# A recurrent cell on one core: GpSimd forms one of the four sums over candidates by halves

## The chip, the cores and the metric

The kernel runs on one core of a Trainium2 chip. The metric is the device time of one execution in microseconds (us). The names of the engines in the profile are PE (TensorE), PEld (its weight loads), DVE (VectorE), ACT (ScalarE), POOL (GpSimd) and SP (SyncE).

## What is computed

A recurrent network runs over 2048 sequences of 256 steps. One step, cut to what matters here:

```
encoded   = tanh(x @ We + state @ Ue + be)
candidate = tanh(x @ Wx[c] + state @ Ws[c] + bk[c])        for c in 0..7, 32 values each
mem       = the last 20 of [encoded, err];  a = relu(mem @ enc_w1 + enc_b1)
h1, c1    = lstm(relu(a @ enc_w2 + enc_b2), h1, c1);  h2, c2 = lstm(h1, h2, c2)
gate      = softmax(h2 @ gate_w + gate_b) * theta + gate * (1 - theta)   (theta from the last 10 errors)
state     = sum over c of gate[c] * candidate[c]
pred      = clamp01(state[-1]);  err = pred - y
```

The change is about the line `state = sum over c`.

## The kernel before

The 2048 sequences are two groups of 1024. A group is eight tiles of 128 sequences, with the 128 on the partitions; a tile is named by a half `hf` (0, 1) and a quarter `q` (0 to 3). Two quarters make a `pair`. A phase works on three items at once: `new`, `cur` and `old`, an item being one step of one group, so 512 items in all. A loop of 51 turns has ten phases a turn. Each engine has its own program with the order of its calls written out by hand in `phase`, and the engines are tied by semaphores alone.

For an old item the new gate is made on VectorE (L781, L788), which writes it to PSUM, and a second time on GpSimd (L908), which writes it to SBUF. Then the products of gate and candidates are formed: VectorE multiplies the four tiles of pair 1 (`mix`, L799), GpSimd the four tiles of pair 0 in two instructions, quarter 1 and quarter 0 (`mix_quarter`, L920). The products lie in `mixed[partition, pair, hf, quarter in pair, 32, 8]` as float32. VectorE forms all four sums over the eight candidates (`mix_sum`, L817), each a reduction of 512 elements to 64 for one `hf` and one `pair`, into `state`. It does them between the parts of the current item's LSTM cells. The last part of its order in a phase reads: product of pair 1; sum (0, 1); first cell's terms (L720) and value (L726); sum (0, 0); the new hidden value in two instructions (L735); sum (1, 0); sum (1, 1); the sum of errors (L696); the second cell's terms (L720) and value (L726); theta (L702); the prediction (L825); the second cell's hidden value (L735); and the softmax.

L720, L726 and L735 read two tensors of SBUF each; L817 reads one; L799 reads one of SBUF and one of PSUM. ScalarE makes the gates' tanh (L561, L566) ahead of L720 and the tanh of the cell's value (L571) between L726 and L735.

TensorE waits for the first cell's hidden value (`q_h[0]`, set by the second L735) before the gate matmuls of the second cell (L417), then runs two history matmuls (L366) and transposes the state (`state_transpose`, L293): once for `hf` 0 and once for `hf` 1, each after the two sums of that half (`q_sum[hf][pair]`).

GpSimd's order in a phase is: gate (L908); product of quarter 1, of quarter 0 (L920); then for the current item `kept_share` (L886), which waits for theta, and `kept_gate` (L893); the new error and the prediction (L947, L956); the low part of the new entry (L926); the weighted exponentials (L900). Its products wait until the sums that read `mixed` pair 0 for the item before are done. GpSimd issues no DMA. The DMAs of the loop are issued from SyncE's queue.

Of the kernel before, what the change touches and what calls it, by code (L numbers as in the profile page):

```python
# [12 lines left out]
MEM, C, S, TRAJ, H, ENC = 20, 8, 32, 24, 16, 64  # L13
P = 128
GROUPS = 2
# [27 lines left out]
def recurrent_kernel(nc, x_l, y_l, y, error0, gate0, w, ident_c, columns_c, ind_c, out):  # L43
    ctx = ExitStack()
    with ctx:
        def sb(name, shape, dt=FP32):
            return ctx.enter_context(nc.sbuf_tensor(name, shape, dt))
# [4 lines left out]
        def sem(name):  # L52
            return ctx.enter_context(nc.semaphore(name))
# [37 lines left out]
        state = sb("state", [P, GROUPS, HF, Q, S])  # L91
# [10 lines left out]
        mixed = sb("mixed", [P, 2, HF, Q // 2, S, C])  # L102
# [36 lines left out]
        q_mulpool = [sem(f"q_mulpool{q}") for q in range(2)]  # L139
# [9 lines left out]
                                    "ring", "predout"))  # L149
        q_out_gate = [sem(f"q_out_gate{c}") for c in range(2)]  # L150
        q_in_high = sem("q_in_high")
        q_sum = [[sem(f"q_sum{hf}_{pair}") for pair in range(2)] for hf in range(HF)]

        block = ctx.enter_context(nc.Block())
# [468 lines left out]
        def _(dve):  # L623
# [186 lines left out]
            def mix_sum(item, hf, pair):  # L810
                g, n, u = item
                if pair == 1:
                    dve.wait_ge(q_mul[1], n + GROUPS)
                else:
                    for q in range(2):
                        dve.wait_ge(q_mulpool[q], n + GROUPS)
                V.tensor_reduce(state[:, g, hf, 2 * pair:2 * pair + 2, :], mixed[:, pair, hf, :, :, :], AX, ALU.add)\  # L817
                    .then_inc(q_sum[hf][pair], 1)
# [13 lines left out]
            def phase(items, extra):  # L832
                new, cur, old = items
                if old:
                    fresh_gate(old)
                    new_gate(old)
                if cur:
                    agent_input(cur, 1)
                if old:
                    mix(old, 1)  # L840
                    mix_sum(old, 0, 1)
                if cur:
                    cell_terms(cur, 0)
                    cell_value(cur, 0)
                if old:
                    mix_sum(old, 0, 0)
                if cur:
                    new_hidden(cur, 0, 0)
                    new_hidden(cur, 0, 1)
                if old:  # L850
                    mix_sum(old, 1, 0)
                    mix_sum(old, 1, 1)
                if cur:
                    error_sum(cur)
                    cell_terms(cur, 1)
                if new:
                    error_rows_wait(new, extra)
                if cur:
                    cell_value(cur, 1)
                    thetas(cur)  # L860
                if old:
                    prediction(old)
                if cur:
                    new_hidden(cur, 1, 0)
                    new_hidden(cur, 1, 1)
                if new:
                    errors(new)
                if cur:
                    peaks(cur)
                    below_peak(cur)  # L870
                    totals(cur)
                    reciprocals(cur)

            run_phases(dve, phase, turn_start)

        @block.gpsimd
        def _(pool):
            G = nc.gpsimd
            G.memset(hist[:, :, :, :].rearrange("p a k b -> p (a k b)").bitcast(FP32), 0.0).then_inc(s_hist0, 1)
            pool.wait_ge(s_ready, 1)  # L880
            pool.wait_ge(s_ys, 16)

            def kept_share(item):
                g, n, u = item
                pool.wait_ge(q_theta, n)
                G.tensor_tensor(one_theta[:, g, :], ones[:, :], theta[:, g, :], ALU.subtract)\  # L886
                    .then_inc(q_onetheta, 1)

            def kept_gate(item):
                g, n, u = item  # L890
                pool.wait_ge(q_onetheta, n)
                pool.wait_ge(q_keptfrom, n)
                G.tensor_tensor(kept[:, g, :, :], gate[:, g, :, :],  # L893
                                one_theta[:, g, :].rearrange("p (j o) -> p j o", o=1)
                                .to_broadcast([P, TILES, C]), ALU.mult).then_inc(q_kept, 1)

            def weighted_exponentials(item):
                g, n, u = item
                pool.wait_ge(q_exp, n)
                G.tensor_tensor(weighted[:, g, :, :], expd[:, g, :, :],  # L900
                                theta[:, g, :].rearrange("p (j o) -> p j o", o=1)
                                .to_broadcast([P, TILES, C]), ALU.mult).then_inc(q_weighted, 1)

            def gate_in_sbuf(item):
                g, n, u = item
                pool.wait_ge(q_fresh, n)
                pool.wait_ge(q_kept, n)
                G.tensor_tensor(gate[:, g, :, :], fresh[:, g, :, :], kept[:, g, :, :], ALU.add)\  # L908
                    .then_inc(q_keptfrom, 1)

            def mix_quarter(item, q):
                g, n, u = item
                pool.wait_ge(q_keptfrom, n + GROUPS)
                pool.wait_ge(q_cand[q], n + 1)

                for hf in range(HF):
                    pool.wait_ge(q_sum[hf][0], n + (GROUPS - 1))
                over_s = gate[:, g, q:Q:2, :].rearrange("p h (o c) -> p h o c", o=1)\
                    .to_broadcast([P, HF, S, C])
                G.tensor_tensor(mixed[:, 0, :, q, :, :], cand[:, g, 0, :, q, :, :], over_s, ALU.mult)\  # L920
                    .then_inc(q_mulpool[q], 1)

            def entry_low(item):
                g, n, u = item
                pool.wait_ge(q_eh, n)
                G.tensor_tensor(entry_parts[:, g, 1, :], entry[:, g, :], entry_parts[:, g, 0, :],  # L926
                                ALU.subtract).then_inc(q_el, 1)

            def place(item, extra):

                g, n, u = item
                if extra is None:
                    return 0, 1
                if extra == "end":
                    return STEPS - 1, STEPS % WINDOW
                step, odd, even = extra
                after = u + 2
                return step + (u + 1), (odd + after if after < PER_TILE else even + (after - PER_TILE))

            def new_error(item, extra):  # L940
                g, n, u = item
                tiles = slice(TILES * g, TILES * g + TILES)
                step, ring = place(item, extra)
                pool.wait_ge(q_pred, n)
                pool.wait_ge(q_errsum, n)
                pred = pred_now[:, g, :].rearrange("p (j o) -> p j o", o=1)
                G.tensor_tensor(err_ring[:, tiles, bass.ds(ring, 1)], pred, ys[:, tiles, bass.ds(step, 1)],  # L947
                                ALU.subtract).then_inc(q_ring, 1)

            def keep_prediction(item, extra):  # L950
                g, n, u = item
                tiles = slice(TILES * g, TILES * g + TILES)
                step, ring = place(item, extra)
                pool.wait_ge(q_pred, n)
                pred = pred_now[:, g, :].rearrange("p (j o) -> p j o", o=1)
                G.tensor_copy(preds[:, tiles, bass.ds(step, 1)], pred).then_inc(q_predout, 1)  # L956

            def turn_start(turn):
                step = pool.snap(turn * PER_TILE)
                odd = pool.snap((turn % 2) * PER_TILE)  # L960
                even = pool.snap((turn + 1) % 2 * PER_TILE)
                return step, odd, even

            def phase(items, extra):
                new, cur, old = items
                if old:
                    gate_in_sbuf(old)
                    mix_quarter(old, 1)
                    mix_quarter(old, 0)
                if cur:  # L970
                    kept_share(cur)
                    kept_gate(cur)
                if old:
                    new_error(old, extra)
                    keep_prediction(old, extra)
                if new:
                    entry_low(new)
                if cur:
                    weighted_exponentials(cur)

            run_phases(pool, phase, turn_start)


# [93 lines left out]
```

## Time and profile before

| | us |
|---|---|
| median of three runs | 5460.53 (5460.39 to 5464.48) |
| the profiled execution | 5460.57 |
| its span, first to last instruction | 5458.7 |
| TensorE busy | 5391.8 |
| VectorE busy | 4479.8 |
| ScalarE busy | 3807.2 |
| GpSimd busy | 2421.7 |

The granted TensorE clock was 0.998 of full over the span. Busy times are those of one profiled execution. Matmuls overlap one another and their ends are modelled, so that a busy TensorE is one whose matmuls leave no gap. A weight load (PEld) can stand waiting while the matmuls before it still stream, so the idle time of PEld is larger than that of PE.

### The profile page before, as it was taken

The page shows a single profiled execution, that of the slowest core. Times are in us where ns is not written, and L with a number is a line of the kernel's source. Part 1 is how long each engine was busy: PE and PEld are TensorE (multiplying, and loading weights), DVE is VectorE, ACT ScalarE, POOL GpSimd, SP SyncE. Part 2 cuts the span into 40 slices and gives each one's busy share as a digit, 9 for nine tenths or more (in the row PEclk, how much of TensorE's full clock was granted, in tenths as well). Part 3 has the DMA queues.
Part 4 walks back from the last instruction along what each step waited for, and adds up shares of the span by engine and source line. Part 5 has one row for each costly group of instructions (what it writes and reads, how often), then busy time and mean ns, then how long its engine had stood idle before and what let it go on. Part 6 is the DMA issues. An engine that isn't in the chain of part 4 may idle for free.

```text
span 5458.7 us, 188210 instructions
## 1 busy us (share of the span) xinstructions
PE 5391.8 (99%) x67584; PEld 3426.0 (63%) x67584; DVE 4479.8 (82%) x12336; ACT 3807.2 (70%) x9729; POOL 2421.7 (44%) x4613
## 2 busy tenths in 40 slices
PE   8999999999999999999999999999999999999998
PEld 5666666666666666666666666666666666666665
DVE  7888888888888888888888888888888888888887
ACT  5777777777767777777777777777777777777775
POOL 3444444444444444444444444444444444444444
PEclk9999999999999999999999999999999999999999
DMA  2111111111111111111111111111111111111111
GB/s 69 29 29 32 29 32 29 32 29 32 29 32 29 32 29 30 31 29 32 29 32 29 32 29 32 29 32 29 30 31 29 32 29 32 29 32 29 32 29 40
DMA packets 299285, 172.38 MB, mean 32 GB/s; under 512 B 156734, under 2 KB 263882, under 8 KB 298714
## 3 DMA queue, kind: packets, MB, share of 16 engines
q1 hardware_dynamic: 293568, 159.42, 11.2%
q8 instruction: 564, 9.24, 0.7%
q10 hardware_dynamic: 5146, 3.66, 0.2%
q14 instruction: 7, 0.06, 0.0%
HBM read 74.65 MB, written 2.10 MB: 14 GB/s over the span
## 4 chain that ended last, share of the span: by engine, by line
PE 95%; DVE 4%; issue 1%; DMA 0%; POOL 0%; ACT 0%; DVEq 0%; ACTq 0%; POOLq 0%
PE a_ps L366 26%; PE chain L417 17%; PE cand_ps L338 9%; PE a_ps L377 9%; PE cand_ps L347 7%; PE chain L310 5%; PE chain L317 4%; PE chain L403 4%; PE chain L293 4%; PE a_ps L388 3%; PE chain L435 3%; PE cand_ps L330 3%; DVE mixed L799 1%; DVE state L817 1%; DVE added L720 1%
## 5 line engine op out<-in xcount | busy, mean ns | idle before, releaser
L366 PE MATMUL a_ps<-hist,w_hist 125*64 125x512 f16 x12288 | 1896.3, 383 | 24.1 <-DMA w_hist<-enc_table 24.1
L817 DVE TENSOR_REDUCE state<-mixed 128x64 f32<-128x512 f32 x2048 | 1353.4, 682 | 34.2 <-POOL mixed L920 0.8
L920 POOL TENSOR_TENSOR mixed<-cand,gate 128x512 f32<-128x512 f32 x1024 | 1281.1, 1272 | 48.6 <-POOL gate L908 12.5
L554 ACT ACTIVATE cand<-cand_ps 128x512 f32<-128x512 f32 x2048 | 1101.8, 593 | 91.1 <-PE cand_ps L347 90.6
L417 PE MATMUL chain<-cell_in,cell_w 128*64 128x128 f32 x16384 | 1120.7, 278 | 19.8 <-DVE cell_in L735 19.8
L886 POOL TENSOR_TENSOR one_theta<-ones,theta 128x8 f32<-128x8 f32 x512 | 103.4, 202 | 2241.0 <-DVE theta L702 2241.0
L417 PEld LDWEIGHTS chain<-cell_in,cell_w 128*64 128x64 f32 x16384 | 889.2, 136 | 271.5 <-DVE cell_in L735 211.8
L366 PEld LDWEIGHTS a_ps<-hist,w_hist 125*64 125x64 f16 x12288 | 681.4, 109 | 536.2 <-issue 141.7
L561 ACT ACTIVATE gates<-chain 128x384 f32<-128x384 f32 x1024 | 502.0, 490 | 726.3 <-PE chain L417 726.1
L735 DVE SCALAR_TENSOR_TENSOR cell_in<-gates,tanh_c 64x128 f32<-64x128 f32 x2048 | 582.5, 284 | 127.0 <-ACT tanh_c L571 113.4
L720 DVE SCALAR_TENSOR_TENSOR added<-gates 128x256 f32<-128x256 f32 x1024 | 537.1, 524 | 141.2 <-ACT gates L561 141.2
L799 DVE TENSOR_TENSOR mixed<-cand,chain 128x1024 f32<-128x1024 f32 x512 | 615.6, 1202 | 0.0
L338 PE MATMUL cand_ps<-w_x,x_sb 32*128 32x256 f32 x8192 | 587.5, 401 | 0.0
L377 PE MATMUL a_ps<-entry,w_now 100*64 100x256 f32 x4096 | 555.7, 390 | 1.4 <-issue 1.2
L926 POOL TENSOR_TENSOR entry_parts<-entry,entry_parts 128x256 f16<-128x256 f32 x512 | 343.5, 671 | 441.5 <-ACT entry_parts L530 441.5
L347 PE MATMUL cand_ps<-w_s,state_t 32*128 32x256 f32 x8192 | 533.4, 374 | 0.0
L571 ACT ACTIVATE tanh_c<-gates 128x128 f32<-128x128 f32 x1024 | 316.6, 309 | 300.8 <-DVE gates L726 300.8
L347 PEld LDWEIGHTS cand_ps<-w_s,state_t 32*128 32x128 f32 x8192 | 420.1, 185 | 22.4
L338 PEld LDWEIGHTS cand_ps<-w_x,x_sb 32*128 32x128 f32 x8192 | 370.3, 184 | 99.2 <-issue 87.9
L403 PE MATMUL chain<-indicator,cell_bias 128*64 128x512 f16 x2048 | 409.4, 380 | 0.0
L536 ACT ACTIVATE a_sb<-a_ps,columns 128x512 f32<-128x512 f32 x512 | 351.7, 687 | 63.1 <-PE a_ps L377 2.8
L770 DVE TENSOR_REDUCE total<-expd 128x8 f32<-128x64 f32 x512 | 112.6, 220 | 303.7 <-ACT expd L586 303.7
(76 smaller groups left out, 6823.8 us busy)
## 6 DMA issues: line engine op xcount, KB each, us to landing
x_sb<-in_x_l SPq DMA_DIRECT2D x260, 256.0 KB, 2.7
hist<-entry_parts SPq DMA_DIRECT2D x2048, 25.0 KB
w_hist<-enc_table SPq DMA_DIRECT2D x258, 128.0 KB, 2.4
y_rows<-in_y_l SPq DMA_DIRECT2D x260, 8.0 KB
ys<-in_y ACTq DMA_DIRECT2D x1, 2048.0 KB, 16.3
preds_out<-preds SPq DMA_DIRECT2D x1, 2048.0 KB, 7.5
cand<-in_encoder ACTq DMA_DIRECT2D x1, 640.0 KB, 3.8
cell_w<-in_cell ACTq DMA_DIRECT2D x2, 256.0 KB, 4.5
```

What stands on the lines that cost most here:

```text
L338: nc.tensor.matmul(cand_ps[q][:, NS * hf:NS * hf + NS], x_sb[rows, x_slot(u), g, P * hf:P * hf + P], w_x[rows, :], start=False, stop=False ...
L347: last = nc.tensor.matmul(cand_ps[q][:, NS * hf:NS * hf + NS], state_t[rows, g, P * hf:P * hf + P], w_s[rows, :], start=False, stop=True, ...
L366: nc.tensor.matmul(a_ps[g][ENC * half:ENC * half + ENC, :], w_hist[0:HROWS, w_slot(u), kk, wp, :], hist[0:HROWS, xp, k, at:at + 512], star ...
L377: last = nc.tensor.matmul(a_ps[g][rows, COLS * p:COLS * p + COLS], w_now[0:ER, p, rows], entry[0:ER, g, :], start=False, stop=True, skip_g ...
L403: nc.tensor.matmul(chain[g][rows, :], cell_bias[:, c, rows], indicator[:, :], start=True, stop=False, skip_group_check=True)
L417: last = nc.tensor.matmul(chain[g][rows, P * r:P * r + P], cell_w[c][:, hf, r, :], cell_in[c][:, g, hf, :], start=False, stop=True, skip_g ...
L554: ins = nc.scalar.activation(cand[:, g, q // 2, :, q % 2, :, :].rearrange("p h s c -> p h (s c)"), cand_ps[q][:, :].rearrange("p (h k) -> ...
L720: V.scalar_tensor_tensor(added[c][:, g, :, :], gates[c][:, g, 1:3, :], 1.0, gates[c][:, g, 3:5, :], ALU.add, ALU.mult).then_inc(q_added[c], 1)
L735: last = V.scalar_tensor_tensor(cell_in[1][rows, g, hf, :], gates[c][rows, g, 0, :], 1.0, tanh_c[c][rows, g, :], ALU.add, ALU.mult)
L799: V.tensor_tensor(mixed[:, 1, :, :, :, :].rearrange("p h l s c -> p (h l) s c"), cand[:, g, 1, :, :, :, :].rearrange("p h l s c -> p (h l) ...
L817: V.tensor_reduce(state[:, g, hf, 2 * pair:2 * pair + 2, :], mixed[:, pair, hf, :, :, :], AX, ALU.add)\
L920: G.tensor_tensor(mixed[:, 0, :, q, :, :], cand[:, g, 0, :, q, :, :], over_s, ALU.mult)\
```

## The change

VectorE's sum of `hf` 1 and pair 0 is taken out of its order. GpSimd forms it instead, right behind its two products, in three additions: the eight candidates are folded to four (256 results per partition) and to two (128 results) in place in `mixed`, and the last two are added into `state` (64 results). Each addition waits for the one before by a semaphore of its own; the last one sets the semaphore that VectorE's sum used to set. VectorE goes on forming the three other sums.

```
+        q_halved = [sem(f"q_halved{k}") for k in range(2)]
...
                 if old:
-                    mix_sum(old, 1, 0)
                     mix_sum(old, 1, 1)
...
+            def half_sum(item, hf):
+                g, n, u = item
+                for q in range(2):
+                    pool.wait_ge(q_mulpool[q], n + GROUPS)
+                terms = mixed[:, 0, hf, :, :, :]
+                for k, (width, then) in enumerate(((C // 2, q_halved[0]), (C // 4, q_halved[1]))):
+                    if k:
+                        pool.wait_ge(q_halved[k - 1], n)
+                    G.tensor_tensor(terms[:, :, :, 0:width], terms[:, :, :, 0:width],
+                                    terms[:, :, :, width:2 * width], ALU.add).then_inc(then, 1)
+                pool.wait_ge(q_halved[1], n)
+                G.tensor_tensor(state[:, g, hf, 0:2, :].rearrange("p l (s o) -> p l s o", o=1),
+                                terms[:, :, :, 0:1], terms[:, :, :, 1:2], ALU.add).then_inc(q_sum[hf][0], 1)
...
                     gate_in_sbuf(old)
                     mix_quarter(old, 1)
                     mix_quarter(old, 0)
+                    half_sum(old, 1)
```

## Rows read from the trace of the kernel before

**Rows 1.** The page: busy time by engine, and the chain that ended last by engine.
```profile
PE 5391.8 (99%) x67584; PEld 3426.0 (63%) x67584; DVE 4479.8 (82%) x12336; ACT 3807.2 (70%) x9729; POOL 2421.7 (44%) x4613
...
PE 95%; DVE 4%; issue 1%; DMA 0%; POOL 0%; ACT 0%; DVEq 0%; ACTq 0%; POOLq 0%
```

**Rows 2.** Three phases by windows: length, then busy time and instructions per engine.
```profile
core 0: us, PE busy (x) PEld busy (x) DVE busy (x) ACT busy (x) POOL busy (x), PEclk, DMA share, GB/s
3001.42:3012.44 11.02, 10.63 (x134) 6.58 (x134) 9.17 (x26) 7.33 (x20) 5.07 (x10) 1.00 0.19 47
3012.44:3022.96 10.52, 10.52 (x134) 6.79 (x134) 8.68 (x26) 7.45 (x20) 4.75 (x10) 1.00 0.04 11
3022.96:3033.45 10.49, 10.49 (x134) 6.58 (x134) 8.64 (x25) 7.44 (x20) 4.68 (x10) 1.00 0.18 50
```

**Rows 3.** Waits: engine and line waited for, total us, times, longest.
```profile
PEld chain L417 <- DVE cell_in L735: 211.8, 510, 0.9
...
PEld chain L293 <- issue: 157.5, 512, 0.8
```

**Rows 4.** Timeline of an ordinary phase: start, length, engine, line, [idle before].
```profile
3012.08 2.51 POOL L920 TENSOR_TENSOR mixed<-cand,gate 128x512 f32<-128x512 f32 x2
...
3014.28 0.59 DVE L720 SCALAR_TENSOR_TENSOR added<-gates 128x256 f32<-128x256 f32 x1
...
3014.91 0.29 DVE L726 SCALAR_TENSOR_TENSOR gates<-added 128x128 f32<-128x128 f32 x1
3015.11 0.68 DVE L817 TENSOR_REDUCE state<-mixed 128x64 f32<-128x512 f32 x1
...
3015.71 0.58 DVE L735 SCALAR_TENSOR_TENSOR cell_in<-gates,tanh_c 64x128 f32<-64x128 f32 x2
...
3016.32 1.28 DVE L817 TENSOR_REDUCE state<-mixed 128x64 f32<-128x512 f32 x2
3016.34 0.85 PEld L417 LDWEIGHTS chain<-cell_in,cell_w 128*64 128x64 f32 x16 [0.39 <-DVE cell_in L735]
...
3017.59 0.46 PE L293 MATMUL chain<-ident,state 128*128 128x128 f32 x2
...
3018.01 0.42 DVE L720 SCALAR_TENSOR_TENSOR added<-gates 128x256 f32<-128x256 f32 x1 [0.27 <-ACT gates L561]
...
3018.92 0.20 POOL L886 TENSOR_TENSOR one_theta<-ones,theta 128x8 f32<-128x8 f32 x1 [4.33 <-DVE theta L702]
...
3019.13 0.59 DVE L735 SCALAR_TENSOR_TENSOR cell_in<-gates,tanh_c 64x128 f32<-64x128 f32 x2 [0.22 <-ACT tanh_c L571]
3019.20 0.38 POOL L893 TENSOR_TENSOR kept<-gate,one_theta 128x64 f32<-128x64 f32 x1
```

**Rows 5.** Timeline of the first phase of a loop turn.
```profile
3001.55 2.50 POOL L920 TENSOR_TENSOR mixed<-cand,gate 128x512 f32<-128x512 f32 x2 [0.24 <-POOL gate L908]
...
3003.26 1.08 DVE L720 SCALAR_TENSOR_TENSOR added<-gates 128x256 f32<-128x256 f32 x1
...
3004.37 0.29 DVE L726 SCALAR_TENSOR_TENSOR gates<-added 128x128 f32<-128x128 f32 x1
...
3005.17 0.58 DVE L735 SCALAR_TENSOR_TENSOR cell_in<-gates,tanh_c 64x128 f32<-64x128 f32 x2
...
3005.81 0.53 PEld L417 LDWEIGHTS chain<-cell_in,cell_w 128*64 128x64 f32 x10 [0.87 <-DVE cell_in L735]
```

**Rows 6.** Groups by line: count, busy us, mean ns, idle before.
```profile
L817 DVE TENSOR_REDUCE state<-mixed 128x64 f32<-128x512 f32 x2048 | 1353.4, 682 | 34.2 <-POOL mixed L920 0.8
...
L926 POOL TENSOR_TENSOR entry_parts<-entry,entry_parts 128x256 f16<-128x256 f32 x512 | 343.5, 671 | 441.5 <-ACT entry_parts L530 441.5
...
L900 POOL TENSOR_TENSOR weighted<-expd,theta 128x64 f32<-128x64 f32 x512 | 150.4, 294 | 1.2 <-ACT expd L586 1.2
...
L947 POOL TENSOR_TENSOR err_ring<-pred_now,ys 128x8 f32 x512 | 130.8, 256 | 2.3 <-DVE pred_now L825 2.3
...
L886 POOL TENSOR_TENSOR one_theta<-ones,theta 128x8 f32<-128x8 f32 x512 | 103.4, 202 | 2241.0 <-DVE theta L702 2241.0
```

## The prediction

> **What bounds the kernel now.** I read the page's first part and the chain that ended last. TensorE is busy 99% of the span and the chain runs through it for 95%; VectorE has 4% [rows 1]. So a shorter VectorE is worth nothing by itself, and a longer one costs only where TensorE comes to stand. Next the windows, cut at the start of VectorE's product (L799) in three consecutive phases: an ordinary phase takes 10.52 or 10.49 us and TensorE is busy in all of it; the first phase of a loop turn takes 11.02 with TensorE busy for 10.63 [rows 2]. The waits say where the tie to VectorE is: before the gates of the second cell (L417) the weight loads sit for 211.8 us in total until the new hidden value (L735) is there [rows 3]. In the timeline of an ordinary phase those loads start at 3016.34, after a stand of 0.39 us, while L735 ends at 3015.71+0.58 = 3016.29 [rows 4]. The matmuls show no gap, since earlier ones were still streaming, but there is no slack left either: whatever ends L735 later ends the phase later.
>
> **A test of this that the trace holds.** In the first phase of a turn L735 ends at 3005.17+0.58 = 3005.75, which is 4.33 us after L799's start at 3001.42; in the ordinary phase it is 3016.29-3012.44 = 3.85. It is 0.48 late, and the phase is 11.02 long against 10.52 and 10.49, so 0.50 to 0.53 more [rows 2, 4, 5]. A delay of L735 passes to the phase at about 1.06 to 1, and nothing later makes it good.
>
> **Why it is late there.** L720, with two inputs in SBUF, takes 0.42 us for the second cell, when GpSimd rests. For the first cell it takes 0.59 in the ordinary phase and 1.08 in the turn's first. In both it ends 0.28 to 0.29 after GpSimd's two products (L920): 3012.08+2.51 = 3014.59 against 3014.28+0.59 = 3014.87, and 3001.55+2.50 = 3004.05 against 3003.26+1.08 = 3004.34 [rows 4, 5]. It stands until GpSimd's product is through and only then moves its 256 elements. L817, with one input, takes 0.68 beside the products as elsewhere [rows 4, 6]. It goes the other way too: L893 on GpSimd takes 0.38 where L900, of the same form, takes 0.29; it started inside the first L735 (3019.13, half of 0.59 for each of the two, so to 3019.42) and ended 0.16 after it [rows 4, 6]. The Trainium skill (SBUF — State Buffer, "Who interferes with whom") says of a two-input VectorE instruction and a GpSimd one that reads SBUF that whichever comes first keeps the shared read interface for its whole length. The rows agree for L720; that L726 and L735 can be held too the trace of before does not show. By a split of bandwidth in place of a lock the additions would cost VectorE perhaps half of what follows, which would give about 5575.
>
> **The change, part by part.**
>
> *Removed:* one of four L817 on VectorE, the first of the pair at 3016.32, 0.68 us alone, about 0.6 of the pair's 1.28 [rows 4, 6]. It stands after L735 and before the other sum of the pair, the sum of errors and the second cell's L720. That L720 stands idle for 0.27 until ScalarE's tanh is there, which waits for TensorE; so the time freed becomes waiting. The transposes that read the sums (L293) begin at 3017.59 and the last L817 ends at 3017.60; only the second transpose needs it, and TensorE shows no gap there. Gain: 0.
>
> *Added:* three GpSimd additions of 256, 128 and 64 results per partition, right behind L920, each with a wait for the one before. No row has in-place additions of halves; the nearest are L926 (256 results, 0.67) and L900 (64 results, 0.29), so 0.38 for 192 more, 0.002 us each [rows 6]. Alone they take 0.67+0.42+0.29 = 1.38, and a start that waits for the operation before costs about 0.08 (L886 ends at 3018.92+0.20, L893 starts at 3019.20 [rows 4]), so 1.6 us. Behind them GpSimd has only L886, which waits for the theta of the next item and starts at 3018.92; there is room for them on GpSimd. The sum they make is wanted at 3017.6 by the transposes; they are done by about 3016.3. On GpSimd's own queue and for the reader of the sum they cost nothing.
>
> *What they lie beside* is the first cell's chain on VectorE: L720, L726 and two L735, all with two SBUF inputs. I go through it with ordinary phase times [rows 4].
> 1. The first addition could start at 3014.59+0.08 = 3014.67, but the waiting L720 has the interface until 3014.87. A 64-result operation that was held ended 0.16 after the holder; with 0.38 for the 192 further results the addition ends at 14.87+0.16+0.38 = 3015.41.
> 2. L726 starts at 3014.91 and now stands until then. L720 needed 0.28 after its release for 256 elements, so L726 with 128 takes 0.15: it ends at 3015.56, where it was 3015.20. That is 0.36 late.
> 3. The second addition is held by L726 and ends at 15.56+0.16+0.13 = 3015.85; the third starts at 3015.93 and ends after 0.29 to 0.38 at 3016.22 to 3016.31.
> 4. The sum L817 behind L726 and ScalarE's tanh shift by 0.36, and the first L735 would end at 3016.00+0.36 = 3016.36. It is held until the third addition is through and ends 0.15 after it, at 3016.37 to 3016.46. That adds 0.01 to 0.10; I take 0.06.
>
> L735 is then 0.42 late. Times 1.06 from the turn's first phase, a phase grows by 0.45 us. The turn's first phase gets the same, since there too the additions follow L720's release. There are 512 such phases (L900 runs 512 times [rows 6]): 512 × 0.45 = 230 us. The profiled execution took 5460.6 us for a span of 5458.7, within 0.1 us of the median of 5460.5, so the forecast is 5460.6+230 = **5690 us**.
>
> *Bounds of what no row shows.* Low: the interface goes to VectorE before every addition. Then the first waits for L726 and ends at 15.20+0.16+0.38 = 3015.74, the second lets the first L735 pass (3016.00) and ends at 3016.29, and only the second L735 is held, to 3016.44: 0.15 late, 0.16 a phase, 512 × 0.16 = 82, so 5543. High: additions over halves step through memory. L947, 8 results with wide steps, takes 0.256 against 0.202 for L886, 8 results side by side [rows 6]; charged wholly to the steps that is 0.007 us a result. For the third addition, 56 results more than eight, it would be 0.38 on top: it ends at about 3016.65 and L735 is 0.75 late, 0.79 a phase, 5865 us. Part of L947's excess is surely the same holding by VectorE that L893 shows, so I stay near L926 and L900. The Trainium skill (GPSIMD Engine Reference, "Performance pitfalls for Q7 kernels") puts about half as much again on each element where the step exceeds 8 bytes, which is so in the third addition alone; by that page the forecast would rise by some 30 us, as an estimate. No row here settles it.
>
> **The rivals.**
> - *A. VectorE slips in between.* The waits between the additions leave gaps of 0.08, and VectorE's instructions use them: the low bound, 5543 us. For it: L720 got in as soon as L920 was through. Against it: L920 and its twin left no gap that L720 could use, and L726 begins only after the first addition has queued.
> - *B. The additions are much slower* than L926's size says, through steps and in-place work, so that L735 is 0.6 to 0.9 late: about 5800 to 5900 us, 5850 as its value. For it L947; against it L926 and L900.
> - *C. No change.* The additions do not hold VectorE at all, because L726 and L735 read too little, and the freed sum hides in waits: 5460 us. L735's steady 0.28 to 0.29 speaks for it only while nothing overlaps it; L893's being held by L735 speaks against it.
> - *D. Faster.* The transposes (L293) wait for the last sum more than shows: their loads sit 157.5 us in total before them with no cause named [rows 3], 0.31 a phase. If the removed sum frees 0.2 of it in each phase and L735 is held for less than that, the time falls; with no holding at all by 512 × 0.2 = 102, to 5358. It decides from a holding below 0.2 us. Against it: TensorE has no gap before L293, and L817's end at 3017.60 comes before the second transpose.
>
> **Chances.** Forecast 0.72, with 5610 to 5770 as its own range (shift 0.28 to 0.57); A 0.09; B 0.11; C 0.04; D 0.04. A difference under about 0.2% (11 us) can't be told from none. Slower takes the forecast, A and B: 0.92; same 0.04; faster 0.04. For the range I leave out C, D and the upper half of B: 5540 to 5820.
>
> **What will show each step.** In the profile after: L726 at about 0.65 us in place of 0.29, beginning as before and ending 0.15 after the first addition; L720 of the first cell as before; the first L735 longer by up to 0.1; L817 1536 times, still at 0.68; additions of about 0.7, 0.5 and 0.3 us, the first two lengthened by standing; the stand of the second cell's weight loads grown by some 0.4 us a phase and gaps of about 0.4 before the matmuls of L417; every other TensorE group unchanged and its clock at full. Ordinary phases of about 10.95 us and turn's first ones of 11.45. The prediction is wrong if L726 stays at 0.29, if L735 is late without a longer phase, or if the gap of TensorE stands before the transposes: then the new sum, not the holding, is late.

## The result, and the profile after

The changed kernel takes 5696.9 us (5695.4 to 5697.5, four runs) against 5460.5 for the kernel before on the same chip: a ratio of 1.0431, 95% interval 1.0413 to 1.0449. The forecast was 5690, so the loss of 236 us was put at 230.

In the changed kernel every line behind the additions is shifted: L720, L726 and L735 of before are L721, L727 and L736 here, L817 is L818, L417 is L418, and GpSimd's products L920 are L934. Its additions are L905 (256 and 128 results) and L908 (64 results).

First the page's first part and the chain that ended last, of the changed kernel:

```profile
PE 5436.0 (95%) x67584; PEld 3390.4 (60%) x67584; DVE 4420.0 (78%) x11824; ACT 3754.5 (66%) x9729; POOL 3185.0 (56%) x6149
...
PE 57%; DVE 34%; issue 8%; DVEq 1%; POOL 0%; DMA 0%; ACT 0%; ACTq 0%; POOLq 0%
```

VectorE is busy for 60 us less than in [rows 1] and yet it has 34% of the chain where it had 4%. GpSimd, which caused the loss, has 0%: the chain does not show who held an instruction that was already running. Three phases by windows, cut at VectorE's product as in [rows 2]:

```profile
3131.00:3142.49 11.49, 10.63 (x134) 6.51 (x134) 9.05 (x25) 7.33 (x20) 6.56 (x13) 1.00 0.18 45
3142.49:3153.45 10.96, 10.59 (x134) 6.71 (x134) 8.56 (x24) 7.33 (x20) 6.23 (x13) 1.00 0.04 11
3153.45:3164.43 10.98, 10.63 (x134) 6.51 (x134) 8.54 (x24) 7.33 (x20) 6.18 (x13) 1.00 0.17 47
```

Each of the three phases is 0.44 to 0.49 us longer than its counterpart, the first of a turn like the others, and the granted clock of TensorE is 1.00 in all. The timeline of an ordinary phase, which answers to [rows 4] (its product L800 starts at 3164.43, that of before at 3012.44; L905 x2 is the first two additions):

```profile
3164.08 2.50 POOL L934 TENSOR_TENSOR mixed<-cand,gate 128x512 f32<-128x512 f32 x2
...
3166.27 0.59 DVE L721 SCALAR_TENSOR_TENSOR added<-gates 128x256 f32<-128x256 f32 x1
...
3166.65 1.27 POOL L905 TENSOR_TENSOR mixed<-mixed 128x256 f32<-128x256 f32 x2
3166.89 0.70 DVE L727 SCALAR_TENSOR_TENSOR gates<-added 128x128 f32<-128x128 f32 x1
3167.51 0.67 DVE L818 TENSOR_REDUCE state<-mixed 128x64 f32<-128x512 f32 x1
...
3168.00 0.30 POOL L908 TENSOR_TENSOR state<-mixed 128x64 f32<-128x64 f32 x1
...
3168.11 0.63 DVE L736 SCALAR_TENSOR_TENSOR cell_in<-gates,tanh_c 64x128 f32<-64x128 f32 x2
3168.77 0.69 DVE L818 TENSOR_REDUCE state<-mixed 128x64 f32<-128x512 f32 x1
3168.80 0.74 PEld L418 LDWEIGHTS chain<-cell_in,cell_w 128*64 128x64 f32 x14 [0.84 <-DVE cell_in L736]
3168.80 0.88 PE L418 MATMUL chain<-cell_in,cell_w 128*64 128x128 f32 x12 [0.36 <-DVE cell_in L736]
```

The reader is to see three things. The first cell's L721 is 0.59 as it was. L727 starts 2.46 us after the product, as before (2.47), but takes 0.70 in place of 0.29: it ends after the first addition and not sooner. The pair of L736 takes 0.63 in place of 0.58 and ends at 3168.74, 4.31 after the product in place of 3.85: 0.46 late. TensorE's matmuls then have a gap of 0.36 before L418, where they had none. The same in sums over the span, from the waits of the changed kernel:

```profile
PEld chain L418 <- DVE cell_in L736: 455.4, 511, 1.4
...
PE chain L418 <- DVE cell_in L736: 209.6, 511, 0.9
...
PEld chain L294 <- issue: 157.6, 512, 0.8
```

The weight loads' stand grew from 211.8 to 455.4 us [rows 3], by 243.6; the matmuls' own gap there went from 19.8 (the page of before) to 209.6, 0.41 a phase. These 190 us, and 44 by which TensorE's busy time grew (5436.0 against 5391.8), make up the longer span. The matmuls themselves take no longer (L418 1120.0 us in all, L417 before 1120.7), so they overlap less. The stand before the transposes (L294) is what it was, 157.6 against 157.5.

### The profile page after: what moved, and what is told of

Same layout as the page of the kernel before. It is cut to its first block, busy times and chain, and to the rows that moved or that the text cites. A ratio compares the mean times of both kernels' runs of the same rounds, so it can differ in the third digit from the quotient of the medians.

```text
span 5693.5 us, 189234 instructions
## 1 busy us (share of the span) xinstructions
PE 5436.0 (95%) x67584; PEld 3390.4 (60%) x67584; DVE 4420.0 (78%) x11824; ACT 3754.5 (66%) x9729; POOL 3185.0 (56%) x6149
## 4 chain that ended last, share of the span: by engine, by line
PE 57%; DVE 34%; issue 8%; DVEq 1%; POOL 0%; DMA 0%; ACT 0%; ACTq 0%; POOLq 0%
PE a_ps L367 23%; DVE state L818 12%; DVE mixed L800 11%; PE chain L418 10%; PE a_ps L378 8%; DVE added L721 5%; DVE cell_in L736 5%; PE chain L318 4%; PE a_ps L389 4%; PE chain L294 3%; PE chain L436 3%; PE chain L404 2%; DVE cell_in L745 1%; DVEq L814 0%; DVE gates L727 0%
## 5 line engine op out<-in xcount | busy, mean ns | idle before, releaser
L418 PE MATMUL chain<-cell_in,cell_w 128*64 128x128 f32 x16384 | 1120.0, 278 | 209.8 <-DVE cell_in L736 209.6
L934 POOL TENSOR_TENSOR mixed<-cand,gate 128x512 f32<-128x512 f32 x1024 | 1281.7, 1272 | 48.6 <-POOL gate L922 12.5
L418 PEld LDWEIGHTS chain<-cell_in,cell_w 128*64 128x64 f32 x16384 | 888.5, 136 | 514.5 <-DVE cell_in L736 455.4
L818 DVE TENSOR_REDUCE state<-mixed 128x64 f32<-128x512 f32 x1536 | 1046.8, 682 | 35.2 <-issue 1.0
L721 DVE SCALAR_TENSOR_TENSOR added<-gates 128x256 f32<-128x256 f32 x1024 | 539.8, 527 | 441.5 <-ACT gates L562 441.5
L736 DVE SCALAR_TENSOR_TENSOR cell_in<-gates,tanh_c 64x128 f32<-64x128 f32 x2048 | 612.0, 299 | 127.0 <-ACT tanh_c L572 113.2
L905 POOL TENSOR_TENSOR mixed<-mixed 128x256 f32<-128x256 f32 (+1 forms) x1024 | 608.3, 594 | 80.3
L800 DVE TENSOR_TENSOR mixed<-cand,chain 128x1024 f32<-128x1024 f32 x512 | 615.5, 1202 | 0.0
L727 DVE SCALAR_TENSOR_TENSOR gates<-added 128x128 f32<-128x128 f32 x1024 | 507.1, 495 | 53.0
```

The costliest lines, as they stand in the source:

```text
L418: last = nc.tensor.matmul(chain[g][rows, P * r:P * r + P], cell_w[c][:, hf, r, :], cell_in[c][:, g, hf, :], start=False, stop=True, skip_g ...
L721: V.scalar_tensor_tensor(added[c][:, g, :, :], gates[c][:, g, 1:3, :], 1.0, gates[c][:, g, 3:5, :], ALU.add, ALU.mult).then_inc(q_added[c], 1)
L736: last = V.scalar_tensor_tensor(cell_in[1][rows, g, hf, :], gates[c][rows, g, 0, :], 1.0, tanh_c[c][rows, g, :], ALU.add, ALU.mult)
L800: V.tensor_tensor(mixed[:, 1, :, :, :, :].rearrange("p h l s c -> p (h l) s c"), cand[:, g, 1, :, :, :, :].rearrange("p h l s c -> p (h l) ...
L905: G.tensor_tensor(terms[:, :, :, 0:width], terms[:, :, :, 0:width], terms[:, :, :, width:2 * width], ALU.add).then_inc(then, 1)
```

## The experiments

Each was run beside the kernel before on the same chip; the differences below are against that run's own median of before (5460.1 to 5462.6). The theory is *holding*: a two-input instruction of VectorE stands while a GpSimd operation that reads SBUF runs, and a late hidden value (the result of the first cell's L735) passes one to one to the phase. The rivals are that GpSimd's work costs wherever it stands, that the new sum comes late, and that the removed sum gives something back.

### All three additions behind the hidden value

```
                     mix_quarter(old, 0)
+                    if cur:
+                        pool.wait_ge(q_h[0], cur[1])
                     half_sum(old, 1)
```

> The changed kernel, but GpSimd's three additions wait for the first cell's hidden value (the second L736), so that none of them runs beside L721, L727 or L736. Holding of the read interface: L727 back at 0.29 us and L736 on time at 3.85 us after VectorE's product. The additions then run from about 3.91 to 5.44 us; the second transpose, which began at 5.31, waits for them some 0.2 us. 5460 + 512 x 0.2 = about 5560 us, with TensorE's gap before the transposes and none before L418. Rival 'GpSimd's work costs wherever it stands': about 5697. Rival 'the sum comes late': later still, above 5697.

Measured: 5597.5 us (ratio 1.025, 1.0234 to 1.0266), 137 us over before. The timeline of an ordinary phase (the product at 3110.95):

```profile
3113.38 0.29 DVE L727 SCALAR_TENSOR_TENSOR gates<-added 128x128 f32<-128x128 f32 x1
...
3114.19 0.57 DVE L736 SCALAR_TENSOR_TENSOR cell_in<-gates,tanh_c 64x128 f32<-64x128 f32 x2
...
3114.84 1.21 POOL L905 TENSOR_TENSOR mixed<-mixed 128x256 f32<-128x256 f32 x2 [1.77 <-DVE cell_in L736]
...
3116.06 0.75 PE L294 MATMUL chain<-ident,state 128*128 128x128 f32 x2
3116.13 0.30 POOL L908 TENSOR_TENSOR state<-mixed 128x64 f32<-128x64 f32 x1
...
3116.48 0.14 PEld L294 LDWEIGHTS chain<-ident,state 128*128 128x128 f32 x1 [0.29 <-POOL state L908]
```

L727 and L736 are back at 0.29 and 0.57, with the same GpSimd work in the kernel. That refutes "wherever it stands". What TensorE waits for moved to the transposes: the second one waits for L908, which ends at 3116.43. From the waits of this run, and then the two loads of the transposes in the kernel before (product at 3012.44):

```profile
PEld chain L294 <- POOL state L908: 144.2, 510, 0.3
```

```profile
3017.58 0.27 PEld L293 LDWEIGHTS chain<-ident,state 128*128 128x128 f32 x2 [0.31 <-issue]
```

Before, the two loads ended at 3017.85 and the second, 0.14 long as here, started at 3017.71, 5.27 us after the product; here it starts at 3116.48, 5.53 after it. That is 0.26 late, and the phase is about 0.27 longer. I had expected 0.20, with a second load that began at 5.31 and a last addition that ended at 5.44 in place of 5.48, so I had this second place 37 us too cheap; the place was the one expected.

### Only the third addition behind the hidden value

```
                 pool.wait_ge(q_halved[1], n)
+                if cur:
+                    pool.wait_ge(q_h[0], cur[1])
```

> The changed kernel, but only the third addition waits for the first cell's hidden value. Holding: the first and second addition hold L727 as before (0.70 us), the first L736 is no longer held (0.33 back to 0.28 us), so 0.045 us a phase less: 5697 - 23 = about 5674 us. Rival 'the sum comes late': the third addition starts some 0.7 us later, so slower than 5697. Rival 'L736 is not held, it only waits for something else': 5697.

Measured: 5665.3 us (1.0375, 1.0361 to 1.0389), 32 less than the changed kernel, 23 expected. So the holding of L736 by the last addition is the smaller part and is real; L736's mean is 284 ns again (299 in the changed kernel), 31 us less in all:

```profile
L736 DVE SCALAR_TENSOR_TENSOR cell_in<-gates,tanh_c 64x128 f32<-64x128 f32 x2048 | 580.8, 284 | 126.7 <-ACT tanh_c L572 113.0
```

The sum was made some 0.8 us later and the kernel was faster: "the sum comes late" plays no part in the changed kernel.

### The additions behind the first cell's value

```
+                    if cur:
+                        pool.wait_ge(q_cell[0], cur[1])
                     half_sum(old, 1)
```

> The changed kernel, but the additions wait for the first cell's value (L727). Holding: L727 on time (0.29 us). The first addition runs from 2.82 to about 3.49 after the product's start and holds the first L736 by about 0.09, the second holds the second L736, which ends at about 4.10 in place of 3.85: 0.25 late, 5460 + 512 x 0.25 = about 5590 us. Rival 'GpSimd's work costs wherever it stands' or 'the sum comes late': 5697 or more.

Measured: 5629.8 us (1.031, 1.0294 to 1.0326), 169 over before where 130 were expected. The timeline of an ordinary phase (product at 3128.04):

```profile
3130.52 0.29 DVE L727 SCALAR_TENSOR_TENSOR gates<-added 128x128 f32<-128x128 f32 x1
...
3130.89 1.20 POOL L905 TENSOR_TENSOR mixed<-mixed 128x256 f32<-128x256 f32 x2 [0.68 <-DVE gates L727]
3131.32 0.92 DVE L736 SCALAR_TENSOR_TENSOR cell_in<-gates,tanh_c 64x128 f32<-64x128 f32 x2
```

L727 is free and now both L736 are held, 0.92 for the pair in place of 0.58. The pair ends at 3132.24, 4.20 after the product, 0.35 late; the time gives 0.33 a phase. It is not a matter of L727 in itself: L736, with two inputs as well, pays where it meets the additions. I had sized it too low by 0.10 because I let the first addition end at 3.49 us and it ended at 3.57, which the first L736 waited out, and the second addition then held the second one.

### The additions without the removal

```
+                    mix_sum(old, 1, 0)
                     mix_sum(old, 1, 1)
...
-                terms = mixed[:, 0, hf, :, :, :]
+                terms = spare[:, :, :, :]
```

> VectorE forms all four sums as before, and GpSimd does its three additions besides, in a spare tile of the same shape whose sums nobody reads. Holding, and a removed sum that is worth nothing: the same as the changed kernel, 5697 us within 10. Rival 'taking the sum off VectorE gave back part of the loss': slower than 5697, by up to 0.6 us a phase, 300 us.

Measured: 5703.9 us (1.0445, 1.0431 to 1.0459), 7 us over the changed kernel. VectorE forms four sums again, and the waits (here L421 is L417 of before and L741 is L735) are those of the changed kernel:

```profile
PEld chain L421 <- DVE cell_in L741: 455.8, 511, 1.4
...
PE chain L421 <- DVE cell_in L741: 209.9, 510, 0.9
```

The whole loss is in what was added: 243 us over before, of which the removed sum gives 7 back in the changed kernel.

### The removal without the additions

The sum of half 1, pair 0 is formed by nobody here (a quarter of the state stays zero). The waits for it, before the second transpose, the prediction and GpSimd's products, are taken out with it.

```
-                for pair in range(2):
+                for pair in range(hf, 2):
                     pe.wait_ge(q_sum[hf][pair], n)
...
-                    mix_sum(old, 1, 0)
                     mix_sum(old, 1, 1)
...
-                for hf in range(HF):
-                    pool.wait_ge(q_sum[hf][0], n + (GROUPS - 1))
+                pool.wait_ge(q_sum[0][0], n + (GROUPS - 1))
```

> The kernel before with VectorE's sum of half 1, pair 0 left out and formed by nobody (a quarter of the state stays zero, so the time is that of a kernel with one sum less). If the removed sum is worth nothing: 5460 us within 10. Rival 'the transposes wait for the last sum': faster by up to 0.2 us a phase, down to 5358.

Measured: 5455.3 us (0.9987, 0.9978 to 0.9996), 7 under before (2 to 12 by the interval). So 2048 sums of 0.68 us became 1536, 350 us of VectorE's work, for 7 us of time. That agrees with the 7 us between the changed kernel and the additions alone. "The transposes wait for the last sum" is refuted: their stand is 157.4 us as before.

### Writes in place of the additions

The three additions become three writes of a constant to spare tiles, which wait for nothing, and the sum is formed by nobody; the last write sets the semaphore of the sum.

```
+                for k, width in enumerate((736, 416)):
+                    G.memset(spare[k][:, 0:width], 0.0).then_inc(q_halved[k], 1)
+                G.memset(spare[2][:, 0:288], 0.0).then_inc(q_sum[1][0], 1)
```

> The changed kernel with the three additions replaced by three writes of a constant to spare tiles, of about the same length (0.7, 0.4 and 0.3 us), at the same place in GpSimd's order; they read nothing of SBUF, and the sum is left out. If it is the reading that holds VectorE: L727 at 0.29 us and 5460 us within 15. If being busy or writing on GpSimd is enough: L727 at 0.6 to 0.7 us and 5650 to 5700.

Measured: 5456.7 us (0.9989, 0.9979 to 0.9998), the same as with nothing in their place. The timeline of an ordinary phase (L722, L728 and L737 are L720, L726 and L735 of before):

```profile
3032.91 0.60 DVE L722 SCALAR_TENSOR_TENSOR added<-gates 128x256 f32<-128x256 f32 x1
3033.15 1.11 POOL L900 MEMSET spare<- 128x736 f32 x2
3033.54 0.29 DVE L728 SCALAR_TENSOR_TENSOR gates<-added 128x128 f32<-128x128 f32 x1
...
3034.18 0.35 POOL L901 MEMSET spare<- 128x288 f32 x1
3034.34 0.58 DVE L737 SCALAR_TENSOR_TENSOR cell_in<-gates,tanh_c 64x128 f32<-64x128 f32 x2
```

GpSimd is as busy at the same place (3033.15 to 3034.53), and the value and the hidden pair take 0.29 and 0.58. It is GpSimd's reading that holds VectorE here, not its being busy and not its writing. That the writes wait for nothing, where the additions wait for one another, does not explain the difference: the single addition of the next section has no other to wait for in its phase, and L726 is held all the same. The Trainium skill (SBUF — State Buffer, "Who interferes with whom") says that a two-input VectorE instruction contends with a GpSimd instruction that reads SBUF and not with one that only writes it; this pair of runs, 5697 against 5457, agrees.

### One addition, of two sizes

Both kernels are the one before with all four sums on VectorE and a single addition in a spare tile that nobody reads, of 256 or of 128 results.

```
+                terms = spare[:, :, :, :]
+                G.tensor_tensor(terms[:, :, 0:S, 0:C // 2], terms[:, :, 0:S, 0:C // 2],
+                                terms[:, :, 0:S, C // 2:C], ALU.add).then_inc(q_spare, 1)
```

(with `0:S // 2` for 128 results).

> The kernel before with all four sums on VectorE, and one addition of 256 results per partition in a spare tile added on GpSimd behind its products, read by nobody. Holding: the value (L727 of the changed kernel) is held until it is through and takes 0.70 us in place of 0.29, the hidden value is 0.40 late and not held itself, 5460 + 512 x 0.40 = 5665 us, as the run in which the third addition waited.

> The same with 128 results: alone 0.40 us long against 0.73, so the value is let go 0.33 earlier: it takes 0.37 us in place of 0.29 and the phase is 0.07 longer, 5460 + 512 x 0.07 = 5496 us. Rival 'each dependent GpSimd operation there costs a fixed amount': half of the loss of the 256 or more, 5560.

Measured: 5669.9 us (1.0384, 1.037 to 1.0398) and 5531.3 us (1.013, 1.0114 to 1.0145). The mean of L732 (L726 of before, the value) runs over both cells, of which the second is always at 0.29. The kernel with 256 results first, then the one with 128:

```profile
L732 DVE SCALAR_TENSOR_TENSOR gates<-added 128x128 f32<-128x128 f32 x1024 | 507.9, 496 | 53.0
...
L909 POOL TENSOR_TENSOR spare<-spare 128x256 f32<-128x256 f32 x512 | 403.8, 789 | 40.2
```

```profile
3075.89 0.52 POOL L909 TENSOR_TENSOR spare<-spare 128x128 f32<-128x128 f32 x1
3076.13 0.43 DVE L732 SCALAR_TENSOR_TENSOR gates<-added 128x128 f32<-128x128 f32 x1
```

One addition of 256 costs 210 us (205 expected), of the 243 that all three cost in the run without the removal. With 128 results L732 takes 0.43 (0.14 more than 0.29), and the kernel 71 us more, which is 0.139 a phase. I had expected 0.07: the held addition ended 0.32 us after the holder and not 0.25. By its time alone this run, 5531, is nearer to the rival's 5560 than to my 5496. What speaks against a fixed price per operation is the pair: one operation costs 210 us with 256 results and 71 with 128, a third and not half or more, and the loss follows L732's length in both: 0.41 and 0.14 us more, 0.410 and 0.139 us a phase.

### The kernel before, with the loop's end elsewhere

The test in the prediction rested on the first phase of a turn, where the chain of the first cell is late. If a delay there passes one to one, then taking it away must pay. VectorE stands 0.40 us before L781 (`fresh_gate`) in that phase alone, behind the reciprocal that ends the turn:

```profile
3000.65 0.23 DVE L781 TENSOR_TENSOR fresh<-weighted,recip 128x64 f32<-128x64 f32 x1 [0.40 <-DVE recip L775]
```

The same order of instructions, with the loop's end before the total:

```
                 if old:
+                    totals(old)
+                    reciprocals(old)
                     fresh_gate(old)
...
                     below_peak(cur)
-                    totals(cur)
-                    reciprocals(cur)
```

> The kernel before, all four sums on VectorE and nothing moved in any engine's order; only the loop's end on VectorE lies before the softmax's total and reciprocal and not after them, where VectorE waits 0.6 us for ScalarE in any case. If a delay of VectorE's first-cell chain passes one to one to the phase: the first phase of each turn falls from 11.02 to about 10.5 us, 51 x 0.5 = 26 us, about 5434 us. Rival 'the first phase is long because of TensorE's own loop end': 5460.

Measured: 5443.3 us (0.9965, 0.9952 to 0.9979), 19 us faster where 26 were expected. The first phase fell from 11.02 to 10.67. In it GpSimd still starts its products late, behind its own loop end, and L720 stands until they are through (VectorE's product at 2992.74):

```profile
2992.52 2.51 POOL L920 TENSOR_TENSOR mixed<-cand,gate 128x512 f32<-128x512 f32 x2 [0.24 <-POOL gate L908]
...
2994.58 0.73 DVE L720 SCALAR_TENSOR_TENSOR added<-gates 128x256 f32<-128x256 f32 x1
```

The products end 2.29 us after VectorE's product where they ended 2.15 after it in the ordinary phase [rows 4], and L720 takes 0.73 in place of 0.59: 0.14 late in both. So GpSimd's loop end was moved too:

```
                 if cur:
+                    entry_low(cur)
                 if old:
+                    weighted_exponentials(old)
                     gate_in_sbuf(old)
...
-                if new:
-                    entry_low(new)
-                if cur:
-                    weighted_exponentials(cur)
```

> The kernel with VectorE's loop end moved, and GpSimd's moved too: before the low part of the entry, where GpSimd waits 0.8 us for ScalarE, and not between the weighted exponentials and the gate. The order of every engine stays. In the first phase of a turn GpSimd's products still began 0.14 later than in the others and let L720 go at 2.30 and not 2.15 us; with that gone the phase falls from 10.67 to about 10.52: 51 x 0.15 = 8 us less, 5435 us. Rival 'the rest of the first phase is TensorE's own': 5443.

Measured: 5434.5 us (0.9952, 0.9938 to 0.9965), 28 us under its own run of before. By windows, the turn's first phase and the one behind it, first with VectorE's end moved, then with both:

```profile
2992.74:3003.41 10.67, 10.62 (x134) 6.57 (x134) 8.82 (x25) 7.44 (x20) 4.87 (x10) 1.00 0.17 49
3003.41:3013.93 10.52, 10.52 (x134) 6.78 (x134) 8.69 (x26) 7.46 (x20) 4.76 (x10) 1.00 0.04 11
```

```profile
2988.30:2998.80 10.50, 10.50 (x134) 6.59 (x134) 8.65 (x26) 7.45 (x20) 4.70 (x10) 1.00 0.19 50
2998.80:3009.32 10.52, 10.52 (x134) 6.78 (x134) 8.69 (x25) 7.45 (x20) 4.76 (x10) 1.00 0.04 11
```

With both moved, the first phase is like any other and TensorE is busy in all of it. This version is faster than both kernels, 0.5% under the one before.

## Why the prediction was right, step by step

- *No slack before L417, and delays pass on.* Right. L736 ends 0.46 late and the three phases read are 0.44 to 0.49 longer; the runs with one addition give 0.410 and 0.139 a phase for 0.41 and 0.14 of holding. I had taken a factor of 1.06 from the first phase of a turn; the runs say 1.0.
- *The removed sum is worth nothing.* Right within 7 us, shown both ways (the removal alone, and the additions alone).
- *The first addition holds L726 by 0.36.* Right in kind, 0.05 short in size: it measured 0.41. The addition waits for L720 as step 1 said, but it ended 0.58 behind it where I had 0.16 + 0.38 = 0.54. In place on halves it is slower than L926: 0.73 us where nothing holds it (in the run with all additions late, the first of L905's two), against 0.67.
- *The second addition is held by L726.* Hardly: it takes 0.40 (1.27 for the pair, less 0.79 and 0.08 between them), as long as in the run with all additions late, and not the 0.5 that I had said. Nothing came of it, since no two-input instruction of VectorE lay between L727 and the first L736.
- *The last addition holds the first L735 by 0.01 to 0.10.* Right: 0.05 by the pair's length, 32 us by the run that took it away.
- *A split of bandwidth* in place of a lock (5575): no. L727 ends 0.15 behind the first addition, as a lock has it, and the loss is the whole one.
- *The sum:* 0.42 × 1.06 × 512 = 228, and 230 with the 0.45 that I had rounded to; measured 0.46 × 1.0 × 512 = 236. Two small misses, a factor too high and a holding too low, cancelled, and the removed sum, put at 0, gave 7 us back, so that 5690 for 5697 is closer than the steps were. The closeness is luck in part.
- *The high bound* has a slip: with the third addition ending at 3016.65 and the first L735 0.15 behind it, L735 is 0.80 late by my own steps and not 0.75, which gives 5895 and not 5865. Nothing hangs on it.
- *Rival A* (VectorE slips in between): no. The first addition had queued behind L720, and it went in front of L727. The third had started before the first L736 and kept it out too.
- *Rival B* (slow through steps): no. The third addition, with single elements 32 bytes apart, took 0.30 against L900's 0.29. The Trainium skill (GPSIMD Engine Reference, "Performance pitfalls for Q7 kernels") has half as much again on each element there; by that the third would have taken some 0.35, as an estimate from that page and the 0.002 us a result of [rows 6]. The trace does not agree.
- *Rivals C and D:* refuted. L727 and L736 are held, by the changed kernel's own timeline and by the runs that move the additions; and the removal alone frees 7 us, not 102.

What stays open is why the first addition ended 0.04 us later behind L720 than the rows of before said: its form, in place on halves, is slower by 0.06 where nothing holds it, but no run here tried the same size in another form behind L720. Nor is it shown why the first phase of a turn gives 1.06 or more where the added holdings give 1.0: with both loop ends moved it fell from 11.02 to 10.50, 0.52 for an L735 that had been 0.48 late.

## What to carry to other kernels

An engine that has time to spare is not free to use. Before moving work to GpSimd, list the VectorE instructions with two SBUF inputs that would run beside it, and see whether one of them sits on the chain that the bounding engine waits for; the work taken off VectorE counted 7 us here, the holding 243. Where a loop's first pass differs from the others, its lateness is a measured test of how a delay passes on, and a place to look for time: moving the loop's end to where the engine waits anyway brought 28 us without changing an instruction or the order of one engine.

## What the runs showed of the hardware beyond the forecast

- A held GpSimd operation ended 0.58 us behind the VectorE instruction that held it with 256 results (3166.86 to 3167.44 in the changed kernel, its length 0.79 by the 256-result run) and 0.32 with 128. The 128 further results made 0.26 of difference there, and 0.33 between the first two additions unheld (0.73 and 0.40 in the run with all additions late, the one of 128 in another shape).
- GpSimd's writes of a constant left the two-input VectorE instructions beside them as they were, at 0.29 and 0.58 us. Whether the writes were slowed is not shown, since no run has them alone.
- The end of the loop cost VectorE a stand of 0.40 us at the next instruction, and GpSimd one of 0.24 before its products. Where the engines were waiting for ScalarE anyway it cost nothing: the turn's first phase took 10.50 us.
